# Key rows of a cross attention: from staging into the stacks by nine direct transfers, or through a scratch in HBM

## What is computed

```python
def _L0_xattn_ref(query, key, value, Wq, Wk, Wv, Wo):
    q = (query @ Wq.T).reshape(B, L, H, D) * scale      # L = 256, H = 16, D = 32
    k = (key @ Wk.T).reshape(B, -1, H, D)               # 25088 rows
    v = (value @ Wv.T).reshape(B, -1, H, D)
    scores = jax.nn.sigmoid(jnp.einsum('blhd,bshd->bhls', q, k))
    o = jnp.einsum('bhls,bshd->blhd', scores, v).reshape(B, L, E)
    return o @ Wo.T
```

## Time and profile before

| | us |
|---|---|
| median of 3 runs | 2237.26 |
| lowest, highest | 2229.64, 2239.34 |
| the profiled execution's own time | 2244.02 |
| its span, first to last instruction | 2242.3 |
| mean granted TensorE clock | 0.969 |

### The profile page before, as it was taken

One profiled execution on the slowest core, in us unless ns is written; L12 is line 12 of the kernel. 1 busy time (PEld: TensorE's weight loads), 2 busy tenths in 40 slices (PEclk: granted clock), 3 DMA queues, 4 the chain that ended last, 5 costly groups with the idle time before them and its releaser, 6 DMA issues. The chain is left out here.

```text
span 2242.3 us, 50143 instructions
## 1 busy us (share of the span) xinstructions
PE 2052.9 (92%) x19340; PEld 1826.1 (81%) x19340; DVE 1224.5 (55%) x2116; ACT 1007.0 (45%) x1129; POOL 26.7 (1%) x31
## 2 busy tenths in 40 slices
PE   7889999899899999989999899898998989987999
PEld 5878888788888788878878788787887878845998
DVE  5655566555666555655556665565646655524422
ACT  3434445344443444434444344443444435432764
POOL 4000000000000000000000000000000000000000
PEclk9999999999999999999999999999999999999999
DMA  5666656666666666666666666666665665543774
GB/s 186 175 184 185 188 177 194 173 176 196 177 198 177 182 187 180 191 178 175 191 178 200 178 180 186 180 191 176 178 184 175 194 177 175 160 165 143 252 275 175
DMA packets 123233, 414.63 MB, mean 185 GB/s; under 512 B 16472, under 2 KB 16472, under 8 KB 91608
## 3 DMA queue, kind: packets, MB, share of 16 engines
q1 hardware_dynamic: 91080, 318.62, 45.9%
q10 hardware_dynamic: 32112, 95.43, 16.4%
HBM read 309.66 MB, written 104.33 MB: 185 GB/s over the span
## 5 line engine op out<-in xcount | busy, mean ns | idle before, releaser
L364 ACT ACTIVATE probs<-sc 128x1024 f32<-128x1024 f32 x784 | 760.6, 1023 | 1008.5 <-PE sc L663 750.8
L631 PE MATMUL kp<-x_combos,weights_r 128*128 128x256 f32 x4116 | 581.2, 293 | 137.6 <-DVE k_parts L494 122.8
L631 PEld LDWEIGHTS kp<-x_combos,weights_r 128*128 128x128 f32 x4116 | 540.9, 200 | 149.3 <-DVE k_parts L494 126.6
L650 PE MATMUL vp<-more_weights,x_combos 128*128 128x256 f32 x3528 | 494.8, 292 | 5.8 <-DVE v L515 4.2
L650 PEld LDWEIGHTS vp<-more_weights,x_combos 128*128 128x128 f32 x3528 | 467.1, 201 | 10.4 <-DVE v L515 5.9
L663 PE MATMUL sc<-rows_r,k_stack_r 96*128 96x256 f32 x3136 | 453.6, 288 | 22.4 <-DMA k_stack_r<-k_rows 20.7
L663 PEld LDWEIGHTS sc<-rows_r,k_stack_r 96*128 96x128 f32 x3136 | 406.7, 193 | 66.4 <-issue 61.9
L678 PE MATMUL acc<-probs,v 128*32 128x256 f32 x6272 | 362.2, 383 | 0.1
L494 DVE TENSOR_TENSOR k_parts<-k_parts,kp 128x512 f32<-128x512 f32 x245 | 168.1, 686 | 300.9 <-PE kp L631 300.5
L678 PEld LDWEIGHTS acc<-probs,v 128*32 128x32 f32 x6272 | 194.3, 110 | 133.0 <-issue 2.1
L476 DVE CAST x_combos<-ctx_raw 128x512 fp32r<-128x512 f32 x235 | 99.4, 423 | 193.4 <-DMA ctx_raw<-ctxT_dram 187.7
(11 more groups left out here) (145 smaller groups left out, 932.0 us busy)
## 6 DMA issues: line engine op xcount, KB each, us to landing
k_stack_r<-k_rows SPq DMA_DIRECT2D x588, 256.0 KB, 5.2
k_rows<-k_rows_hi SPq DMA_DIRECT2D x196, 256.0 KB
k_rows<-k_rows_lo SPq DMA_DIRECT2D x196, 256.0 KB
ctx_raw<-ctxT_dram ACTq DMA_DIRECT2D x47, 1024.0 KB, 12.2
piece<-w_all_dram ACTq DMA_DIRECT2D x176, 256.0 KB, 8.6
w_raw<-w_all_dram SPq DMA_DIRECT2D x44, 1024.0 KB, 4.8
weights<-wqk_dram SPq DMA_DIRECT2D x2, 1024.0 KB, 13.2
rows_r<-q_rows SPq DMA_DIRECT2D x3, 512.0 KB, 7.9
```

Of the source, the lines that this page charges most:

```text
L364: nc.scalar.activation(probs[:, t % 2, g, :], sc[g % 2][:], ACT.Sigmoid).then_inc(probs_ready, 1)
L631: last = nc.tensor.matmul(k2[:, r, :], wk[i - 1][:, k, a, r * P:(r + 1) * P], xc[:, i - 1, k, b, :], start=i in FRESH and n == 0, stop=n = ...
L650: last = nc.tensor.matmul(v2[:, r, :], xc[:, i - 1, k, b, r * P:(r + 1) * P], wv_c[i - 1][:, k, a, :], start=i in FRESH and n == 0, stop=n ...
```

## The change

The scratch in HBM and its five transfers in a quarter go. In their place are nine: four transfers of 64 KB carry the high rows of one head each from the staging (32 partitions, 2 KB each) to partitions 0 to 31 of the stack, four carry the low rows to partitions 32 to 63, and one of 256 KB copies the high rows from partitions 0 to 31 of the stack to 64 to 95. The SP queue now works quarter by quarter: it waits for the high part, issues four, waits for the low part, issues four, waits until the four high ones have landed and issues the copy. The waits for the score tiles on the SP queue go but for one (all of chunk c's tiles, ahead of the copy of quarter 2). Staging slots come free when the direct transfers have landed. TensorE waits for the low rows and for the copy.

```diff
-            def keep_rows(m, q):
-                at = q % 2
-                sp.wait_ge(k_hi, m * 3 + q)
-                sp.dma_start(kept[q, 0].rearrange("d j r n -> j d r n"), f32(kr_hi[:, at, :, :])).then_inc(hi_kept[q], 16)
-                sp.wait_ge(k_lo, m * 3 + q)
-                sp.dma_start(kept[q, 1].rearrange("d j r n -> j d r n"), f32(kr_lo[:, at, :, :])).then_inc(lo_kept[q], 16)
-
-            def stack_rows(m, q):
-                i, j = QUADRANT[q]
-                to = f32(kst[:, j, i, :, :, :])
-                sp.wait_ge(hi_kept[q], m * 16 + 16)
-                sp.dma_start(to[0:D], kept[q, 0]).then_inc(stacked[q], 16)
-                sp.dma_start(to[2 * D:3 * D], kept[q, 0]).then_inc(stacked[q], 16)
-                sp.wait_ge(lo_kept[q], m * 16 + 16)
-                sp.dma_start(to[D:2 * D], kept[q, 1]).then_inc(stacked[q], 16)
+            def stack_rows(m, q, free=False):
+                i, half = QUADRANT[q]
+                to, at = f32(kst[:, half, i, :, :, :]), q % 2
+                if q == 0:
+                    sp.wait_ge(k11_hi, m + 1)
+                else:
+                    sp.wait_ge(k_hi, m * 3 + q)
+                for j in range(HG):
+                    sp.dma_start(to[0:D, j, :, :], f32(kr_hi[D * j:D * (j + 1), at, :, :])).then_inc(hi_moved[q], 16)
+                if q == 0:
+                    sp.wait_ge(k11_lo, m + 1)
+                else:
+                    sp.wait_ge(k_lo, m * 3 + q)
+                for j in range(HG):
+                    sp.dma_start(to[D:2 * D, j, :, :], f32(kr_lo[D * j:D * (j + 1), at, :, :])).then_inc(lo_moved[q], 16)
+                if q == 2 and free:
+                    sp.wait_ge(scores_ready, m * (TC * G))
+                sp.wait_ge(hi_moved[q], m * MOVED + MOVED)
+                sp.dma_start(to[2 * D:3 * D], to[0:D]).then_inc(hi_twice[q], 16)
...
                 if k_next:
-                    keep_first(m)
-                    sp.wait_ge(scores_ready, c * (TC * G) + 4)
-                    stack_rows(m, 0)
-                    keep_rows(m, 1)
-                    keep_rows(m, 2)
-                    sp.wait_ge(scores_ready, c * (TC * G) + 8)
-                    stack_rows(m, 1)
-                    keep_rows(m, 3)
-                    sp.wait_ge(scores_ready, c * (TC * G) + 12)
-                    stack_rows(m, 2)
-                    sp.wait_ge(scores_ready, c * (TC * G) + 16)
-                    stack_rows(m, 3)
+                    for q in range(4):
+                        stack_rows(m, q, True)
...
-                        dve.wait_ge(hi_kept[1], m * 16 + 16)
-                        dve.wait_ge(lo_kept[1], m * 16 + 16)
+                        dve.wait_ge(hi_moved[1], m * MOVED + MOVED)
+                        dve.wait_ge(lo_moved[1], m * MOVED + MOVED)
...
-                    pe.wait_ge(stacked[{(0, 0): 0, (0, 2): 1, (2, 2): 2, (2, 0): 3}[t, g]], c * STACKED + STACKED)
+                    q = {(0, 0): 0, (0, 2): 1, (2, 2): 2, (2, 0): 3}[t, g]
+                    pe.wait_ge(lo_moved[q], c * MOVED + MOVED)
+                    pe.wait_ge(hi_twice[q], c * 16 + 16)
```

More of the change, by code:

```diff
@@ L103, in keep_clock, with cross_attention @@
         nc.tensor.matmul(to, zeros[:, 0:P], zeros[:], start=True, stop=True, skip_group_check=True)
-def cross_attention(nc, x, ctxT, wqT, wkT, wvT, woT, wqk, wv, bv, wo, w_all, kept, kept_q, keep):
+def cross_attention(nc, x, ctxT, wqT, wkT, wvT, woT, wqk, wv, bv, wo, w_all, kept_q, keep):
     ident, x1, qst, next_weights = keep["ident"], keep["x1"], keep["rows"][0], keep["weights"][1]
@@ L174, in cross_attention @@
         k_sum, k_hi, k_lo = sem("k_sum"), sem("k_hi"), sem("k_lo")
-        hi_kept, lo_kept = [sem(f"hi_kept{q}") for q in range(4)], [sem(f"lo_kept{q}") for q in range(4)]
-        stacked = [sem(f"stacked{q}") for q in range(4)]
+        hi_moved, lo_moved = [sem(f"hi_moved{q}") for q in range(4)], [sem(f"lo_moved{q}") for q in range(4)]
+        hi_twice = [sem(f"hi_twice{q}") for q in range(4)]
         v_made, vt_saved, v11_saved, v_sum = sem("v_made"), sem("vt_saved"), sem("v11_saved"), sem("v_sum")
@@ L184, in cross_attention @@
         SCALE = float(D) ** -0.5
-        STACKED = 3 * 16
+        MOVED = HG * 16
         def quarter(w, i, j):
@@ L376, in k_first @@
                 if not first:
-                    act.wait_ge(hi_kept[2], m * 16)
+                    act.wait_ge(hi_moved[2], m * MOVED)
                 nc.scalar.activation(kr_hi[:, 0, :, :], k2, ACT.Copy).then_inc(k11_hi, 1)
@@ L486, in k_first_rest @@
                 if not first:
-                    dve.wait_ge(lo_kept[2], m * 16)
+                    dve.wait_ge(lo_moved[2], m * MOVED)
                 nc.vector.tensor_tensor(kr_lo[:, 0, :, :], k2, f32(kr_hi[:, 0, :, :]), ALU.subtract).then_inc(k11_lo, 1)
@@ L498, in k_summed @@
                     if q == 2:
-                        dve.wait_ge(hi_kept[0], m * 16 + 16)
-                        dve.wait_ge(lo_kept[0], m * 16 + 16)
+                        dve.wait_ge(hi_moved[0], m * MOVED + MOVED)
+                        dve.wait_ge(lo_moved[0], m * MOVED + MOVED)
                     elif q == 3:
-                        dve.wait_ge(hi_kept[1], m * 16 + 16)
-                        dve.wait_ge(lo_kept[1], m * 16 + 16)
+                        dve.wait_ge(hi_moved[1], m * MOVED + MOVED)
+                        dve.wait_ge(lo_moved[1], m * MOVED + MOVED)
                     elif not first:
-                        dve.wait_ge(hi_kept[3], m * 16)
-                        dve.wait_ge(lo_kept[3], m * 16)
+                        dve.wait_ge(hi_moved[3], m * MOVED)
+                        dve.wait_ge(lo_moved[3], m * MOVED)
                     nc.vector.tensor_copy(kr_hi[:, at, :, :], to).then_inc(k_hi, 1)
@@ L1302, in build @@
         keep["v"] = rows[:, 2, :, :].rearrange("p g l -> p (g l)").rearrange("p (a n) -> p a n", a=LT)
-        kept = nc.dram_tensor("k_rows", (4, 2, D, HG, 2, HS), F32, kind="Internal").ap()
         kept_q = nc.dram_tensor("q_rows", (2, D, HG, G, L), F32, kind="Internal").ap()
-        cross_attention(nc, x, ctxT, wqT, wkT, wvT, woT, wqk, wv, bv, wo, w_all, kept, kept_q, keep)
+        cross_attention(nc, x, ctxT, wqT, wkT, wvT, woT, wqk, wv, bv, wo, w_all, kept_q, keep)
         keep |= {"any_inexact": sb("any_inexact", [1, 1], mybir.dt.int32), "inexact_ready": sem("any_inexact_ready"),
```

## The result

The changed kernel takes 2024.24 us (median of 4 runs, 2022.42 to 2025.13), against 2238.3 us before on the same chips: a ratio of 0.905, 95% interval 0.9025 to 0.9074. The forecast was 2034 us, with 2010 to 2130 as its range. The profiled execution took 2024.77 us, its span is 2023.1 us; the one of before took 2244.02.

What follows compares the result with a forecast made beforehand. TensorE was taken to bound the kernel, with holes from the late raw load. 47 intervals falling from 39.86 to 35.7 us give 195.5, plus 5 and 3 at the ends: 2034 us against the median, range 2010 to 2130.

Steps and rivals of the forecast that it cites:

- The bound, and what the load is worth: Raw load's late landing sets TensorE's hole at keys(6), slot waits lie beside it; intervals 39.86 us against a 35.40 floor.
- The 9.0 us: Raw load must be usable 9.0 us after its issue for keys(6) to start undisturbed; it took 12.62.
- Short holes cost no clock: TensorE in the loop: the 0.3 us of hole left in each interval would not lower the granted clock.
- VectorE starts L476 8 to 9 us after L430's issue: Sign of being right: VectorE's first use of the raw load comes 8 to 9 us after the load's issue.
- The four engines: Scratch writes, four heads outermost, run on four of 16 DMA engines and hold the raw load there 3.3 us or more.
- The size of the load's landing: Raw load in the changed kernel: lands in 8.4 + 0.3 = 8.7 us, leaving 0.3 us of hole per interval.
- the moves of quarter 0 take the place of quarter 3's reads in the window of the load, so I leave its rate as it is: Traffic beside the raw load: replaced like for like, so it lands when twelve engines finished before, 8.4 us after issue.
- My bound from below, 5 to 6 us: Raw load's quickest landing: (1.0 + 0.75) MB at 424 GB/s plus about 1 us.
- The ends: TensorE's waits outside the loop: 5 us won at the start, 3 at the end.
- The SP queue: 36 transfers a chunk at 0.30 to 0.65 us, 10.8 to 23.4 us of 35.7, fit; added waits don't end on TensorE.
- The load improves by half: Rival: small SBUF moves slow the mixture, load usable after 10.5 or 11.3 us; 2090 or 2128 us, chance 0.20.
- Transfers that cannot overlap: Rival: each of 36 transfers holds the SP queue; slower from 1.11 us each, 2394 us at 1.2, chance 0.08.

Runs made afterwards that it cites:

- small_load: The kernel before with each raw load inside the loop cut from 1 MB to its first 64 KB; 2066.44 us in one run.
- load_behind_1: The changed kernel with one 1 MB HBM-to-HBM copy issued on ScalarE's queue ahead of each raw load inside the loop; 2081.48 us in one run.
- scratch_heads: The kernel before with each 256 KB scratch write cut into four of 64 KB, one for each head; 2023.91 us in one run.
- scratch_even: The kernel before, HBM scratch and five transfers a quarter kept, but the scratch laid out with the 128 staging rows outermost; 2021.95 us.
- ballast_four: The changed kernel plus the two old 256 KB writes a quarter, four heads outermost, into a scratch nobody reads; 2455.5 us.
- ballast_sixteen: The changed kernel plus two 256 KB writes a quarter into an unread scratch, with the 128 rows outermost; 2028.11 us.
- halves: The changed kernel with each of a quarter's eight moves cut in two of 32 KB, 68 transfers in a chunk; 2448.99 us in one run.
- order_only: The kernel before with only the SP queue's order changed to quarter by quarter, writes still on four engines; 2387.32 us in one run.

## Why the prediction was right, point by point

**The bound, and what the load is worth: right.** TensorE's holes went with the load's lateness, the slot waits beside it, 223 us in small_load, were worth at most 42 us with the late stacks and the ends in it, and the undisturbed chunk of 35.40 us was the floor: 35.43 us on average. The clock followed: 1.00 in the 47 intervals where the earlier trace rows have 0.97.

**The 9.0 us: right.** small_load (8.0 us, no hole) and load_behind_1 (9.8 us, a hole) lie on either side of it, and both kernels that land the load later have the holes that it gives: 9.8 us less the 0.84 us by which keys(6) was late is about 9.0, and 12.9 less 3.7 (1027.24 against the 1023.56 at which keys(6) was due) is 9.2. "Short holes cost no clock" held for the granted clock, but a short hole cost more than its length (load_behind_1). And the sign "VectorE starts L476 8 to 9 us after L430's issue" came true by luck: 8.06 us is when VectorE gets there by its own order; the load had been there for over 2 us.

**The four engines: right, but not the way in which they held the load.** Three pairs of kernels differ in the slowest dimension of the writes: before and scratch_heads (2238 and 2024; also four times as many writes), before and scratch_even (2022; also another layout, read in rows of 2 KB), ballast_four and ballast_sixteen (2455 and 2028; nothing but the pattern). The prediction put 128 KB of quarter 0's writes beside the load on each of the four. In the packets around the load of the earlier trace rows those writes move only from 1878 on, when the load's last packet is through at 1878.3; and the second plateau of the earlier trace rows, from 1039, starts when that chunk's load is through (1038.9). What the load met on the four engines was quarter 3: the end of its low write, until 1870, and then its reads. What stands in the plateaus behind the load is quarter 0's writes, which came last.

**The size of the load's landing: the term that was off.** I took 8.7 us, from the twelve engines that were done at 8.4, and left 0.3 us of hole in each interval; it was 5.7 us and no hole. The row was misread. All engines were busy until 1876, but not with the load: by its packets the first 96 of 128 were done 3.9 us after the first (median), about 5 us after the issue. What kept the twelve engines busy until 1876 was mostly quarter 3's reads. So the step that failed is that "the moves of quarter 0 take the place of quarter 3's reads in the window of the load, so I leave its rate as it is". Those reads stood in that window only because the writes before them were late: once the writes are fast, quarter 3 is through 8 us before the load goes out. My bound from below, 5 to 6 us, was nearer, in part by luck: its 424 GB/s were not reached (265 from 951 to 957), no row stands behind its "about 1 us", and the 0.75 MB that it adds were not all in the window. Price: 208.5 us won in the intervals less the 195.5 forecast, 13 us.

**The ends: together 10.7 us for the 8 forecast**, but otherwise shared: 3.8 for 5 at the start, 6.9 for 3 at the end. Of the latter 5.65 us are two waits for a stack in the last chunk, the 3.56 us of the earlier trace rows and one of 2.09 at 1985.12, both gone in the changed kernel. The prediction counted the first alone.

**The SP queue: right.** 36 transfers at 0.61 us lie inside the 0.30 to 0.65 us; the slots cost VectorE 9.0 us in all, 8.0 of them in the first chunk; SP's added waits for the high moves (133.5 us in all, 48 times, 5.1 us at most) stopped nobody in the loop. The SP queue moved 102.7 MB less, as said.

**The sum.** The forecast against the profiled execution was 2040.5 us and it took 2024.8: 15.7 us, of which 13.0 are the load and 2.7 the ends. Against the median the error is 9.8 us. That it is smaller is luck: I took 6.8 us off because the profiled execution of before stood that far over its median, and that of the changed kernel stands only 0.5 us over its own.

**The rivals.** None occurred. "The load improves by half" rested on 32-partition traffic slowing the mixture; the load with nine small moves beside it ran at a share of 0.86 and 265 GB/s and was in time. "Transfers that cannot overlap" had the right sum (the time that SP is held for each transfer) and the wrong reason for it: in halves it is the issue that holds SP, while the transfers overlap. The fixed parts did not follow one another: a move of 64 KB took 2.0 to 2.3 us to land, yet a quarter was through SP in 5.7 us (966.29 to 972.00), far from the 19.8 us of the prediction's estimate.

**What the change did not need.** The route was not at fault. The diff takes HBM out of the way and raises the transfers of a quarter from five to nine; the same time is had by turning the scratch's slowest dimension from 4 to 128, with five. As an argument for the change "direct in place of through HBM" would have been the wrong lesson, and the prediction, which put the gain on the four engines, did not say so plainly enough to expect it.

## What to carry to other kernels

Here a DMA share that stood still at a quarter, with 25 GB/s for each engine in it, was a transfer whose pattern had an outermost dimension of four: with such a plateau look at the patterns before the route, the sizes or the order. That all engines are busy does not say with what: before a time is read from it, ask whose packets they are. Ask of a late load by when it must be there, in us after its issue, and compare that with its landing; the room is what a change gives or takes. When a transfer is made fast, everything that was late behind it moves too, so don't keep its old company in the estimate; and count the issues of a queue against the period of the loop before cutting transfers smaller.

## What the runs showed of the hardware that was not expected

- Writes of 256 KB with four heads outermost took 7.3, 9.6 and (beside a 1 MB load) 13.9 us to land, the same bytes from 128 rows outermost 3.1 us, four of 64 KB from 32 rows each 2.2 to 2.5 us each.
- A load of 64 KB took 8.0 us to land beside the four-engine writes, a load of 1 MB 5.3 to 6.4 us without them and 6.1 us in order_only, where they had landed before it went out: landing time told of the traffic beside it, not of the size.
- Of a load of 1 MB held in this way three quarters of the packets were done after 3.9 us and the last after 10.0; undisturbed 3.0 and 4.1.
- The issue of a write on SP took 0.52 us with the heads outermost and 0.32 to 0.34 us with the 128 rows outermost. A move of 32 rows took 0.60 to 0.62 us, whether of 64 KB or of 32 KB.
- Copies within the SBUF of 32 partitions and 256 KB landed in 3.0 us, the moves of 64 KB in 2.0 to 2.3 us, though they were issued 0.6 us apart and so three or four were in flight at a time.
